# First attention in four quadrants of the array, rank products early, routing in pairs of tiles, and a new order at two joints

## What is computed

```
x = x + attention0(layernorm(x), ctx)       # attention over the 64 rows, per head of 64 columns
x = x + experts(layernorm(x))               # top 2 of 8 experts, relu, mean of the two
x = x + attention1(layernorm(x), ctx)       # 32 query heads, 8 key/value heads
x = x + ffn(layernorm(x))                   # silu(gate) * up, then down

# attention0, for each sequence b and each of 8 heads h (D = 64 rows, L = 512, Lh = 64)
q, k, v = W @ x + bias                      # W is 64 x 64 and acts on the rows
p  = softmax(q_h k_h^T / sqrt(64))          # 64 x 64
out = Wo @ concat_h(p v_h) + bo

# experts: logits = x @ W_gate + b_gate; the two largest experts of each row
```

## Time and profile before

| | us |
|---|---|
| median of 3 runs (906.70 to 908.38) | 906.88 |
| the profiled execution | 911.67 |
| its span | 909.7 |
| first attention and routing, up to the first load of the experts | 174.7 |
| experts, up to the first sum of the expert rows | 142.4 |
| second attention and feed forward | the rest |

### The profile page before, as it was taken

How to read it: one execution, slowest core, us unless ns; L and a number is a source line. 1 busy time by engine, 2 the same in 40 slices (tenths; PEclk the granted TensorE clock), 3 DMA queues, 4 the chain that set the end, 5 groups by cost and what they waited for, 6 DMA issues and landing times.

```text
span 909.7 us, 19693 instructions
## 1 busy us (share of the span) xinstructions
PE 864.2 (95%) x7537; PEld 705.6 (78%) x7537; DVE 443.7 (49%) x900; ACT 347.6 (38%) x567; POOL 292.9 (32%) x412
## 2 busy tenths in 40 slices
PE   5999998699999979999999899999999999999997
PEld 4787887678888967777777778887888788878885
DVE  3988886434444567888888831223122221222112
ACT  3555663233333345676666542221222122211111
POOL 3587875200000387777764131112020002002000
PEclk9999998799999989999999899999999999999999
DMA  8556555588444262554421531110030003002001
GB/s 284 178 186 225 213 202 191 188 276 300 163 163 151 96 225 74 166 152 139 142 75 48 149 116 36 46 44 0 13 104 24 0 12 104 1 8 85 1 1 46
DMA packets 55084, 105.24 MB, mean 116 GB/s; under 512 B 8050, under 2 KB 12146, under 8 KB 54866
## 3 DMA queue, kind: packets, MB, share of 16 engines
q1 hardware_dynamic: 48226, 84.98, 28.6%
q0 software_dynamic: 5120, 16.78, 5.5%
q10 hardware_dynamic: 1648, 2.23, 0.7%
HBM read 67.99 MB, written 35.98 MB: 114 GB/s over the span
## 4 chain that ended last, share of the span: by engine, by line
PE 73%; ACT 2%; DMA 2%; issue 2%; DVE 1%; SPq 0%; POOL 0%; DVEq 0%; ACTq 0%; POOLq 0%
PE c_ps L1231 9%; PE c_ps L1233 9%; PE c_ps L1232 9%; PE c_bank L1746 4%; PE c_bank L1269 3%; PE c_bank L1747 3%; PE c_bank L1270 3%; PE c_bank L1751 3%; PE c_bank L1275 3%; PE c_bank L1807 3%; PE c_ps L1782 2%; PE c_bank L982 2%; PE c_bank L983 2%; PE c_bank L988 2%; PE c_po L982 2%; PE c_po L983 2%
## 5 line engine op out<-in xcount | busy, mean ns | idle before, releaser
L1308 DVE SCALAR_TENSOR_TENSOR d_hid<-c_ps,d_b_up,d_silu 128x512 f32<-128x512 f32 (+1 forms) x44 | 33.0, 750 | 228.6 <-PE c_ps L1233 228.6
L1231 PE MATMUL c_ps<-d_nT_hi,gate_up_hi 128*128 128x512 f32 (+1 forms) x352 | 139.9, 398 | 0.0
L1233 PE MATMUL c_ps<-d_nT_hi,gate_up_lo 128*128 128x512 f32 (+1 forms) x352 | 138.6, 394 | 0.0
L1232 PE MATMUL c_ps<-d_nT_lo,gate_up_hi 128*128 128x512 f32 (+1 forms) x352 | 138.3, 393 | 0.0
L1187 ACT ACTIVATE d_silu<-c_ps,d_b_gate 128x512 f32<-128x512 f32 (+1 forms) x44 | 30.3, 689 | 141.3 <-PE c_ps L1233 141.3
L1147 POOL TENSOR_TENSOR late_x<-late_x,d_b_down 128x512 f32<-128x512 f32 x16 | 21.2, 1356 | 188.2 <-DMA late_x<-x_after_attention 188.2
L1233 PEld LDWEIGHTS c_ps<-d_nT_hi,gate_up_lo 128*128 128x128 f32 (+1 forms) x352 | 65.2, 185 | 16.5
L1232 PEld LDWEIGHTS c_ps<-d_nT_lo,gate_up_hi 128*128 128x128 f32 (+1 forms) x352 | 65.4, 186 | 15.8
L1231 PEld LDWEIGHTS c_ps<-d_nT_hi,gate_up_hi 128*128 128x128 f32 (+1 forms) x352 | 65.3, 185 | 15.4
L1194 ACT ACTIVATE d_hid_hi<-d_hid 128x512 fp32r<-128x512 f32 (+1 forms) x44 | 27.8, 632 | 126.0 <-DVE d_hid L1308 126.0
L1001 ACT ACTIVATE b_rowsT_hi<-c_bank 128x512 fp32r<-128x512 f32 x39 | 23.4, 600 | 83.7 <-PE c_bank L971 83.7
(11 more groups left out here) (297 smaller groups left out, 1981.5 us busy)
## 6 DMA issues: line engine op xcount, KB each, us to landing
b_rows<-expert_rows SPq DMA_DIRECT2D x39, 256.0 KB, 2.8
expert_results<-b_result SPq DMA_DIRECT2D x39, 256.0 KB, 2.5
a_wstage<-L_ffn_W_e SPq DMA_DIRECT2D x16, 512.0 KB, 3.8
late_x<-x_after_attention SPq DMA_DIRECT2D x28, 256.0 KB, 3.9
c_stage<-gate_up SPq DMA_DIRECT2D x16, 344.0 KB, 3.4
out<-late_x SPq DMA_DIRECT2D x16, 256.0 KB, 2.8
x_after_attention<-late_x SPq DMA_DIRECT2D x12, 256.0 KB, 3.8
c_y_in<-x_after_attention SPq DMA_DIRECT2D x12, 256.0 KB, 2.7
```

The source lines that it names most:

```text
L1231: pe.matmul(bank[0:w, :], gu_hi[:, cols], nT_hi[:, g % 2, k, :], start=k == 0, stop=False)
L1232: pe.matmul(bank[0:w, :], gu_hi[:, cols], nT_lo[:, g % 2, k, :], start=False, stop=False)
L1233: mm = pe.matmul(bank[0:w, :], gu_lo[:, cols], nT_hi[:, g % 2, k, :], start=False, stop=k == KD - 1)
```

## The change

**Quadrants.** `make_scores` and `make_attn` write some products to the other half of the rows, so that all four quadrants are used: scores go to half `r ^ b` and bank `b`, weighted values of heads 4 to 7 to half `b ^ 1`. The banks `ps` and `pt` become one tensor `pst` of two banks. Heads of sequence 1 thereby stand in swapped order in the transposed probabilities, which `make_attn` undoes, and the heads 4 to 7 of `attn` have their two sequences swapped, which a second weight `wo_cross` undoes in `project`: one product of 512 columns becomes two of 256. `wo_cross` is one more buffer to clear and two more small DMAs at the start.

**Pairs.** Tiles 0 to 11 are routed in six groups of two, the last four singly. `scatter` comes a round later (`m - 5`). `make_rank` moves ahead of `transpose_probs` in rounds below 16. `low_part` waits for the marks of the groups that end up to tile `m - 3`; in rounds 15 and 16 `scale_x1` goes ahead of `low_part`.

**Last rounds.** `keep_kv`, `clear_kv_stage` and the late keys and values stand elsewhere, mostly later; four of the eight are now behind the count instead of two and a half.

**Second joint.** `high_weights(0)` goes ahead of the last `rectify`, `high_weights(1)` right behind it, and both `low_weights` ahead of `keep_values`.

```diff
-    GROUPS = tuple((t, 1) for t in range(TILES))
+    GROUPS = tuple((t, 2) for t in range(0, TILES - 4, 2)) + tuple((t, 1) for t in range(TILES - 4, TILES))
...
+                for half in range(2):
+                    sp.dma_start(wo_cross[64 * half:64 * half + 64, 64 - 64 * half:128 - 64 * half], a["Wo"]).then_inc(o_consts, 16)
...
-            for m in range(-2, TILES + 4):
+            for m in range(-2, TILES + 5):
                 if tile(m + 2):
                     scale_x(m + 2)
-                if tile(m - 4):
-                    scatter(m - 4)
+                if tile(m - 5):
+                    scatter(m - 5)
+                if m >= TILES - 1 and tile(m - 1):
+                    scale_x1(m - 1)
                 if tile(m - 1):
+                    if tile(m - 3):
+                        pool.wait_ge(both_ready, groups_until(m - 2))
                     low_part(m - 1)
+                if m < TILES - 1 and tile(m - 1):
                     scale_x1(m - 1)
...
+                            at = 64 * (r ^ b)
-                            mm = pe.matmul(ps[rows, cols], qT[rows, cols], kT[rows, cols], start=True, stop=True)
+                            mm = pe.matmul(pst[at:at + 64, b, 64 * j:64 * j + 64], qT[rows, cols], kT[rows, cols], start=True, stop=True)
...
+                            h, rows, at = n + 4 * cross, slice(64 * b, 64 * b + 64), 64 * (b ^ cross)
+                            mm = pe.matmul(po[at:at + 64, cross, 65 * n:65 * n + 65], probT[rows, 64 * (h ^ b):64 * (h ^ b) + 64],
...
-                pe.matmul(pvy[:, :], wo[:, :], attn[:, :], start=True, stop=True).then_inc(y_made, 1)
+                pe.matmul(pvy[:, 0:256], wo[:, :], attn[:, 0:256], start=True, stop=True)
+                pe.matmul(pvy[:, 256:512], wo_cross[:, :], attn[:, 256:512], start=True, stop=True).then_inc(y_made, 1)
...
+                if group_ending(m - 3) is not None and m < TILES:
+                    make_rank(group_ending(m - 3))
                 if tile(m):
                     transpose_probs(m)
...
+            if b == BLOCKS + 1:
+                act.wait_ge(y_made, BLOCKS)
+                in_front_of_last(act)
             if b >= 2:
                 rectify(b - 2)
```

More of the change, by code:

```diff
@@ L363, in _ @@
         def _(pool):
-            for buf in (wk, wv, wq, wo):
+            for buf in (wk, wv, wq, wo, wo_cross):
                 pool.memset(buf[:, :], 0.0).then_inc(zeroed, 1)
@@ L568, in make_attn @@
                 want(pe, o_kept, t)
-                for h in range(H0):
-                    for b in range(2):
-                        rows = slice(64 * b, 64 * b + 64)
-                        mm = pe.matmul(po[rows, h // 4, 65 * (h % 4):65 * (h % 4) + 65], probT[rows, 64 * h:64 * h + 64],
-                                       v[rows, t % 2, h, :], start=True, stop=True)
+                for n in range(H0 // 2):
+                    for cross in range(2):
+                        for b in range(2):
+                            h, rows, at = n + 4 * cross, slice(64 * b, 64 * b + 64), 64 * (b ^ cross)
+                            mm = pe.matmul(po[at:at + 64, cross, 65 * n:65 * n + 65], probT[rows, 64 * (h ^ b):64 * (h ^ b) + 64],
+                                           v[rows, t % 2, h, :], start=True, stop=True)
                 mm.then_inc(o_made, 1)
@@ L679, in _ @@
             pe.matmul(pr[:, 0:8], ones[:, :], seenb[:, :], start=True, stop=True).then_inc(count_made, 1)
-            make_late_v(5)
-            for i in range(6, KV_LATE):
+            for i in range(4, KV_LATE):
                 make_late_k(i)
@@ L861, in _ @@
                     keep_attn(m)
+                if m == TILES - 1:
+                    for i in range(3):
+                        clear_kv_stage(i)
             steps = [0]
@@ L1966, in _ @@
             ex.vector(dve)
-            keep_values(0)
             low_weights(0)
-            keep_values(1)
             low_weights(1)
-            keep_values(2)
-            keep_values(3)
+            for t in range(4):
+                keep_values(t)
             add_first_rows()
```

74 lines of the change are left out of this document (35 added, 39 removed).

## The result

The changed kernel takes 904.43 us (median of 20 runs, 900.59 to 908.76), the kernel before 908.49 (20 runs, 904.83 to 910.79). The ratio is 0.9959 with a 95% interval of 0.9945 to 0.9973. By the ratio it is 3.7 us faster (2.5 to 5.0), by the two medians 4.1, where 11.0 were forecast. The forecast also stood on a median of before that was 1.6 us low (906.88). The two profiled executions differ by 5.0 us of span.

The account below looks back on a forecast made before the run. It took PE and POOL, both at 7.91 us per round, as the bounds. Start -2.0, rounds 5 to 14 -4.3, tail -3.8 and joint -0.9 gave -11.0: 895.9 us from the 906.88 median, range 889.0 to 904.0.

Parts of the forecast that it names:

- Start and rounds 0 to 4: First stage's start: two more DMAs cost 1.0 us, faster products gain 0.45 and 2.55; sum -2.0 us.
- 1.0 us for the two loads: At the start, SP's two more DMA issues ahead of tile 2's loads cost 1.0 us, between 0 and 2.8.
- Rounds 5 to 14: First stage: PE needs 7.06 us, POOL 7.91, so POOL bounds; 82.6 falls to 78.3, -4.3 us.
- Rival B: Rounds 5 to 14: POOL's queue has give and PE's 7.06 us holds; -17.7 us, 889.2; chance 0.08.
- C: Quadrants don't run together, PE's round is 7.96 us; only routing, tail and joint gain: -6.4, 900.5; chance 0.15.
- Tail: From tile 15's scores to the experts' first load: 6.9 us less, 3.1 added for the clock; -3.8 us.
- walk: Step-by-step timing from tile 15's scores at full clock: count at 21.0 us, experts' first load at 32.0, before 38.9.
- clock term: In the tail, 3.1 us added for two or three spells of reduced clock after PE gaps.
- Joint: Second joint: DVE's low part ahead of the gathers gains 0.9 and 0.3, last relu loses 0.3; -0.9 us.
- Rival E: Slower: PE idles more and the clock falls to 1.2 GHz each round; +7.6 us, 914.5; chance 0.08.
- Rival D: DVE's blocked marks and late loads keep rounds at 8.2 us, tail gives 2; about -5.5, 901.4; chance 0.09.
- blocked picks: DVE's rank picks fall into POOL's low part: up to 2.4 us of DVE lost per pair, costing nothing unless coinciding.

Follow-up runs that it names:

- late keys moved: Changed kernel with PE's first late keys moved from ahead of tile 15's weighted values to behind tile 13's logits; ratio 1.0001 to the kernel before.
- late keys and scatters: Changed kernel with PE's first late keys behind tile 13's logits and the scatters of tiles 12 to 15 one round earlier on POOL; ratio 0.9998.
- cross loads later: Changed kernel with the two loads of the cross copy of Wo moved on SP behind the context load of tile 2; ratio 0.9941.
- old joint: Changed kernel with the old order at the second joint; ratio 0.9986 to the kernel before.
- early weights: Changed kernel with late key and value weights loaded two rounds earlier: 0.9925; plus later cross Wo loads: 0.9916; plus scatters of tiles 12 to 15 earlier: 0.9893.
- quadrants alone: Kernel before with only the quadrants added; routing, scatters, tail and joint as before; ratio 1.0041.
- wait for the search with epsilon on DVE: Changed kernel with POOL's scatter behind DVE's expert search and marks, and both epsilon additions per round moved from POOL to DVE; ratio 1.0022.
- epsilon on DVE alone: Changed kernel with the addition of epsilon moved from POOL to DVE, twice a round; ratio 1.0039 to the kernel before.

## Why the forecast was wrong

- **Start and rounds 0 to 4**, forecast -2.0: the trace has -1.2, its repetition 53.23 - 51.14 = -2.1. Six executions with this start and these rounds have tile 5 at 51.14 to 52.76, -1.2 in the mean. About 0.8 too much; the 1.0 us for the two loads lies within the 0.4 to 1.6 found.
- **Rounds 5 to 14**, forecast 78.3 us with POOL as the floor. Nine executions have the changed kernel's rounds, but for a load in three of them (the changed one twice, late keys moved, late keys and scatters, cross loads later, old joint, and the three with early weights). They take 78.18 to 82.38 us, 79.5 in the mean; the longest had two maxima held behind a scatter. The mechanism is right, for POOL had no gap but 0.3 us in ten rounds, and the gain was forecast about 1 us too large. What the forecast did not see is that DVE's chain lies close under POOL's floor. Rival B is refuted by the 7.88 us of POOL, C by the 0.62 us of the scores.
- **Tail**, forecast -3.8, measured +0.1, and 39.0 to 41.9 us in ten kernels with quadrants and the changed tail. This is the step that failed, with 3.9 of the 6.0 us by which the profile misses the sum, and it failed in two places.
  - *The load.* The walk put "one late group, 0.89" at 4.8 us behind the scores of tile 15 and did not ask when its weights land. They are released 2.2 us ahead of those scores and landed 6.6 behind them. The wait of 2.62 us then brought the half clock: by the two rows at 0.50 and 0.67, 4 x 0.5 + 4 x 0.33 = 3.3 us of PE's work. The forecast had 3.1 for spells of the clock, and over the whole tail, in stretches of 4 us, the granted clock was short of full by 5.3 us in all, with PE idle or not. The last copy started at 33.7 us, in the repetition at 36.0, where the walk and the clock term gave 28.5 + 3.1 = 31.6.
  - *The end.* The walk ended the stage with ACT's last copy plus 3.5 us and had no scatter in it. The last scatter's landing ended it, and the first load came 5.3 us behind the copy's start: 1.8 more.
  - With the weights there, the last copy came at 29.0 and 27.1 us and the count at 19.2 and 19.3 (forecast 21.0). The tails of 34.3 and 34.8 lie near the forecast's 35.1 in part by luck: PE was earlier than forecast by 2.6 and 4.5 us, and the scatter took back 1.8 and 4.2. The late weights were PE's longest wait there in the changed kernel and its repetition (2.73, besides 2.29 for the exponent); in five of the ten kernels PE stood 2.6 to 3.75 us for the exponent of tile 15 at this place, and for the late keys 0.9 us or less. The forecast had such a gap (2.7).
- **Joint**, forecast -0.9: -1.0 against before at the first sum, -0.9 against the old joint. At the first scores of the second attention only 0.3 is left against before (22.67 and 22.93), 1.5 against the old joint in the new kernel. Right at its place, unsure behind it.
- **Rival E**, the clock, was given a mechanism of its own in every round. In the profiled rounds 5 to 14 of the changed kernel the clock stayed at 1.00, so it did not decide. But it took the gain from two variants (quadrants alone, and the wait for the search with epsilon on DVE), and in the tail it added to the wait. With epsilon on DVE alone the clock stayed at 1.00 in the rounds, and held maxima took the gain. **Rival D**'s blocked picks are there and cost nothing, as forecast:

```profile
95.14 2.38 POOL L414 TENSOR_TENSOR expert_lo<-a_wstage,expert_hi 128x1024 fp32r<-128x1024 f32 x1
...
96.39 1.19 DVE L803 TENSOR_TENSOR a_picked<-a_hot_kept,a_rank 128x32 f32<-128x32 f32 x1
97.50 0.15 DVE L806 TENSOR_TENSOR a_seenb<-a_seenb,a_marks 128x8 bf16<-128x8 bf16 x1
```

## What to carry to other kernels

When engines get faster, re-date every load whose release hangs on their progress: set the landing time, not the issue, beside each step of a walk, and look at the memory traffic in that stretch. If a product comes to stand ahead of its load, load earlier into a buffer that has fallen free rather than move the product. A wait that PE could afford can cost twice as much once the clock falls behind it. Walk every queue to the end of a stage, not only the one that ended it before: here POOL's scatters took over from ACT's copies as soon as PE got faster.

## What the hardware showed that I had not expected

- **A reduction from PSUM can be held by a scatter.** In 20 profiled executions some 60 maxima came up (scores made, DVE free) behind a scatter that POOL had started, or with it. 22 of them started 0.5 to 2.5 us late, 16 of them 0.55 to 0.7 us behind the second scatter's end; the others started at once. Of more than 170 that came up ahead of the scatter none was late. So the order is a condition, but not the whole cause, and what else decides stays open. The Trainium skill (SBUF — State Buffer, Who interferes with whom) says of `tensor_reduce` that on trn2 it "never contends"; the 2.72 us above speak against relying on it, though no run shows that the ports, of which that section speaks, are what held it.
- **The clock falls after short gaps at some places and not at others.** In rounds 5 to 14 five gaps of 0.82 to 1.04 us lay ahead of the projection, and behind four of them it stood at 0.50 to 0.55; behind gaps of 1.1 to 1.9 us ahead of the transposed probabilities it stayed at 1.00 more than ten times. The length of a gap alone does not tell it; ahead of the projection lie the logits, with 8 columns each, and the scores.
- **The same load took 4.9 to 8.3 us to land.** The late value weights, 256 KB, landed after 5.3 us before the change, after 8.3 in the changed kernel, its repetition and the one with the old joint, after 7.2 with the cross loads later, and after 4.9 to 6.2 in four other variants. What decides is open.
